# Swin attention half on Trainium2: values twice, V with the projection, centred x with key and variance

## What is computed

```python
def swin_block_fn(x, shift, mask, ...):
    y = layer_norm(x, ln1_g, ln1_b)                       # rolled by -shift, cut into windows
    qkv = wins @ qkv_w + qkv_b
    attn = softmax(q @ k.T * hd ** -0.5 + bias + mask)    # per window and head, 49 x 49
    out = (attn @ v) @ proj_w + proj_b                    # windows back into the image
    x = x + out
    z = layer_norm(x, ln2_g, ln2_b)
    return x + gelu(z @ fc1_w + fc1_b) @ fc2_w + fc2_b
# then, on 4 groups of 16 channels: covariance, 5 Newton steps, out = gamma * wm @ (x - mu) + beta
```

## Time and profile before

| | |
|---|---|
| median of 3 runs | 780.66 us (780.63 to 780.93) |
| profiled execution: time, span | 782.55 us, 780.8 us |
| TensorE busy (matmul) | 693.6 us, 89% |
| TensorE weight loads | 414.3 us, 53% |
| VectorE busy | 534.0 us, 68% |
| ScalarE busy | 357.8 us, 46% |
| POOL busy | 205.0 us, 26% |
| chain that ended last, TensorE's share | 36% |
| attention halves | about 66 to 305 us and 403 to 640 us |

### The profile page before, as it was taken

The page is one execution under the profiler, slowest core; times in us unless marked ns, Lnnn a source line. Parts: engine busy times, 40 slices in busy tenths (PEclk is TensorE's granted clock), DMA queues, the critical chain, the costliest instruction groups (busy, mean ns, idle before and its releaser), DMA issues. The chain is left out here.

```text
span 780.8 us, 27044 instructions
## 1 busy us (share of the span) xinstructions
PE 693.6 (89%) x11574; PEld 414.3 (53%) x11574; DVE 534.0 (68%) x919; ACT 357.8 (46%) x628; POOL 205.0 (26%) x505
## 2 busy tenths in 40 slices
PE   3766999899999998899768999999999987999778
PEld 2633556556666655343334566666566553434557
DVE  1744797788888865787456898887798555782123
ACT  2512455445545544675434455455355444764200
POOL 4000022123222112346500231231122124797000
PEclk9866999999999999999978999999999998999859
DMA  9200121112112111000000121121121110000004
GB/s 228 46 21 21 36 65 55 54 57 68 59 58 69 56 58 38 23 1 1 21 21 25 57 74 54 58 75 52 53 68 61 58 39 23 2 1 1 2 21 144
DMA packets 47627, 37.56 MB, mean 48 GB/s; under 512 B 28564, under 2 KB 47124, under 8 KB 47508
## 3 DMA queue, kind: packets, MB, share of 16 engines
q1 hardware_dynamic: 46496, 33.96, 14.9%
q10 hardware_dynamic: 1012, 1.87, 0.8%
HBM read 18.15 MB, written 4.01 MB: 28 GB/s over the span
## 5 line engine op out<-in xcount | busy, mean ns | idle before, releaser
L423 POOL TENSOR_TENSOR att<-osb,rec 128x392 f32<-128x392 f32 x64 | 71.1, 1111 | 365.5 <-DMA rec<-dens 365.5
L812 DVE TENSOR_REDUCE nmax<-psum 113x16 f32<-113x784 f32 x128 | 117.6, 959 | 42.7 <-PE psum L1024 42.5
L532 ACT ACTIVATE pt<-psum 113x784 f32<-113x784 f32 x128 | 98.6, 824 | 90.5 <-PE psum L1024 90.5
L1024 PE MATMUL psum<-bt,rows_r 117*113 117x392 f32 x256 | 79.0, 409 | 3.9 <-DVE nmax L812 1.2
L838 DVE RECIPROCAL rpk<-dpk 64x49 f32<-64x49 f32 x64 | 28.9, 452 | 53.6 <-DMA dpk<-osb 53.1
L1024 PE MATMUL psum<-pt,vbd 113*32 113x49 f32 x4096 | 59.8, 209 | 3.8 <-ACT osb L539 3.6
L491 ACT ACTIVATE lv<-psum,epsc 128x392 f32<-128x392 f32 x32 | 18.8, 588 | 96.8 <-PE psum L1024 95.6
L416 POOL TENSOR_TENSOR xl<-XW,xh 128x392 fp32r<-128x392 f32 x24 | 31.9, 1329 | 108.3 <-ACT xh L499 108.3
L1024 PE MATMUL psum<-kexp,qsb 32*49 32x196 f32 x2048 | 59.8, 341 | 0.5 <-DMA kexp<-ksb 0.5
L1024 PEld LDWEIGHTS psum<-pt,vbd 113*32 113x32 f32 x4096 | 50.7, 110 | 15.6 <-issue 14.5
L383 POOL TENSOR_TENSOR XW<-XW,wcol 128x49 f32<-128x49 f32 (+5 forms) x200 | 55.3, 314 | 11.8 <-DVE XW L911 11.6
(11 more groups left out here) (174 smaller groups left out, 1221.9 us busy)
## 6 DMA issues: line engine op xcount, KB each, us to landing
rec<-dens SPq DMA_DIRECT2D x64, 196.0 KB
kexp<-ksb SPq DMA_DIRECT2D x128, 49.0 KB
qexp<-qsb SPq DMA_DIRECT2D x128, 49.0 KB
XW<-x_dram SPq DMA_DIRECT2D x14, 196.0 KB, 4.6
out_dram<-XW SPq DMA_DIRECT2D x14, 196.0 KB, 2.4
dpk<-osb SPq DMA_DIRECT2D x64, 12.2 KB
dens<-rpk SPq DMA_DIRECT2D x64, 12.2 KB, 2.6
pt<-w_dram ACTq DMA_DIRECT2D x2, 384.0 KB, 7.6
```

The source lines that it names most:

```text
L423: nc.gpsimd.tensor_tensor(att[:, 4 * part:4 * part + 4, :], osb[part][:, :].rearrange("p (a n) -> p a n", a=4), rec[part][:, :].rearrange( ...
L532: nc.scalar.activation(pt[grp][:, b:b + 2, :], SC[0:KROWS, b:b + 2, 0:BANK], ACT.Exp)\
L812: nc.vector.tensor_reduce(nmax[:, b:b + 2, grp, :], SC[0:KROWS, b:b + 2, 0:BANK].rearrange("p a (k m) -> p a k m", m=NTOK), AX.X, ALU.max, ...
L1024: return nc.tensor.matmul(o, a, b, start=start, stop=stop, **k)
```

## The change

TensorE's `step` gets a new order: `scores_t` part 0, `pv(G-1, 0)` into `bB`, `pv(G-1, 1)` into `bO`, `scores(G+1, 0)`, `f_v(G+1)`, `proj(G-2)` (now in `bO`), `scores(G+1, 1)`, centred x, key, variance, `scores_t` part 1, `maxt`, query (now in `bO`). So the values of part 0 wait for the next step, with a third exponential buffer (`pt_of`). ScalarE makes both output copies behind the exponentials of part 0 and the query's copy behind those of part 1; the variance's copy follows the key's. VectorE takes the row maxima of part 0 before both reciprocals. SP issues both gathers, both stores and both loads in pairs. At the end of the attention half both values of half 15 use `bO`. The projections of the last two halves name `bO`, which is the bank that they had. The numbers of matmuls, their operands and results are the same. Left out of the diff are the bank names in `residual` and the last projections, and the call sites that `f_k` and `f_q` replace in the starts, where the query waits for `rx_done` as before and stays in `bB`.

```diff
@@ -70,7 +70,8 @@
 XW = [sb("XW0", [128, HALVES * TOK]), sb("XW1", [128, HALVES * TOK])]
-ptb = sb("pt", [128, 2, TILES4, BANK])
+ptb = sb("pt", [128, 3, TILES4, BANK])
 ptflat = ptb[:].rearrange("p g b n -> p (g b n)")
@@ -150,7 +151,11 @@
 rx = sb("rx", [128, 2 * GWIN, NTOK], F32R)
-pt = [ptb[0:KROWS, i] for i in range(2)]
+pt = [ptb[0:KROWS, i] for i in range(3)]
+def pt_of(g, grp):
+    return pt[1 if grp else 2 * (g % 2)]
 osb = [sb(f"osb{i}", [128, 4 * NROWS]) for i in range(2)]
@@ -324,16 +329,17 @@
             if G > base:
-                gather(G - 1, 1)
-                to_rows(G - 1, 0)
-                from_rows(G - 1, 0)
-                to_rows(G - 1, 1)
-                from_rows(G - 1, 1)
+                for part in range(2):
+                    gather(G - 1, part)
+                for part in range(2):
+                    to_rows(G - 1, part)
+                for part in range(2):
+                    from_rows(G - 1, part)
             if G + 2 < base + HALVES:
...
                 spread_q(G + 2)
-            gather(G, 0)
         G = base + HALVES - 1
+        gather(G, 0)
         to_rows(G, 0)
@@ -512,7 +518,7 @@
             act.wait_ge(qexp_in[1 - buf], 64 * spread)
-        nc.scalar.activation(qsb[:, :], bB[:, 0:TOK], ACT.Identity, bias=p["vec"][:, QB:QB + 1])\
+        nc.scalar.activation(qsb[:, :], (bB if g1 % HALVES < 2 else bO)[:, 0:TOK], ACT.Identity, bias=p["vec"][:, QB:QB + 1])\
             .then_inc(q_done, 1)
@@ -524,47 +530,47 @@
-    def expo(g, grp, first=False):
+    def expo(g, grp):
         act.wait_ge(st_ready, 2 * g + grp + 1)
-        if not first:
-            act.wait_ge(av_ready, 2 * (g - 1) + grp + 1)
+        if grp and g:
+            act.wait_ge(av_ready, 2 * g)
+        elif g > 1:
+            act.wait_ge(av_ready, 2 * g - 3)
         for b in (0, 2):
-            nc.scalar.activation(pt[grp][:, b:b + 2, :], SC[0:KROWS, b:b + 2, 0:BANK], ACT.Exp)\
+            nc.scalar.activation(pt_of(g, grp)[:, b:b + 2, :], SC[0:KROWS, b:b + 2, 0:BANK], ACT.Exp)\
                 .then_inc(exp_done, 1)
-    def o_copy(g, part, first=False):
+    def o_copy(g, part, bank):
         act.wait_ge(av_ready, 2 * g + part + 1)
-        if not first:
+        if g:
             act.wait_ge(att_done, 2 * (g - 1) + part + 1)
-        nc.scalar.activation(osb[part][:, :], bO[:, 0:4 * NROWS], ACT.Copy).then_inc(osb_done, 1)
+        nc.scalar.activation(osb[part][:, :], bank[:, 0:4 * NROWS], ACT.Copy).then_inc(osb_done, 1)
...
         f = first and base == 0
-        expo(G, 0, f)
+        expo(G, 0)
         if first:
...
         else:
-            o_copy(G - 1, 1, base == 0 and g == 1)
+            o_copy(G - 1, 0, bB)
+            o_copy(G - 1, 1, bO)
         if ahead > 0:
...
             square(G + 3)
-            variance(G + 3, 1 - u)
         if ahead > 1:
             evac_k(p, G + 2, f)
-            evac_q(p, G + 2, u, (G + 1) // 2 + 1)
+        if ahead > 2:
+            variance(G + 3, 1 - u)
         if g + 1 + AHEAD < HALVES:
             x_high(base // HALVES, g + 1)
-        if tail and ahead > 0:
-            tail[1]()
-        expo(G, 1, f)
-        o_copy(G, 0, f)
-        if tail and ahead == 0:
-            tail[1]()
+        expo(G, 1)
+        if ahead > 1:
+            evac_q(p, G + 2, u, (G + 1) // 2 + 1)
@@ -638,10 +644,12 @@
         step(p, base, HALVES - 2, 0, False, 1, pair=PAIRS - 1,
-             tail=[lambda: stats_of(0, m_copy, m_square), lambda: m_variance(0)])
+             tail=[lambda: stats_of(0, m_copy, m_square, m_variance)])
         step(p, base, HALVES - 1, 1, False, 0,
-             tail=[lambda: stats_of(1, m_copy, m_square), lambda: m_variance(1)])
-        o_copy(base + HALVES - 1, 1)
+             tail=[lambda: stats_of(1, m_copy, m_square)])
+        o_copy(base + HALVES - 1, 0, bO)
+        m_variance(1)
+        o_copy(base + HALVES - 1, 1, bO)
         nxt = base + HALVES
@@ -848,10 +856,10 @@
         else:
-            recip(G - 1, 0, blk == 0 and g == 1)
             if ahead > 0:
                 rowmax(G + 1, 0)
-            recip(G - 1, 1, blk == 0 and g == 1)
+            for part in range(2):
+                recip(G - 1, part, G == 1)
         if g > 1:
@@ -1038,12 +1046,14 @@
-    def f_qk(p, g1, buf, free=None):
+    def f_k(p, g1, buf):
...
         mm(bA[:, 0:TOK], p["wk"][:, :], z[buf][:, :]).then_inc(k_ready, 1)
-        pe.wait_ge(*(free or (rx_done, g1)))
-        mm(bB[:, 0:TOK], p["wq"][:, :], z[buf][:, :]).then_inc(q_ready, 1)
+    def f_q(p, buf, bank):
+        mm(bank[:, 0:TOK], p["wq"][:, :], z[buf][:, :]).then_inc(q_ready, 1)
@@ -1098,36 +1108,35 @@
-    def pv(g, grp, buf, first=False):
+    def pv(g, grp, buf, bank):
...
             pe.wait_ge(v_done, 2 * g + 2)
-        if not first:
-            pe.wait_ge(osb_done, 2 * g + grp)
         for win in range(GWIN):
...
                     c0 = (2 * win + hg) * NTOK
-                    last = mm(bO[32 * h4:32 * h4 + 32, c0:c0 + NTOK],
+                    last = mm(bank[32 * h4:32 * h4 + 32, c0:c0 + NTOK],
                               vbd[buf][:, (GWIN * grp + win) * HEADS + 4 * hg + h4, :],
-                              pt[grp][:, h4, c0:c0 + NTOK])
+                              pt_of(g, grp)[:, h4, c0:c0 + NTOK])
         last.then_inc(av_ready, 1)
-    def proj(p, g, bank=bA):
+    def proj(p, g):
...
                 for w in range(2):
-                    last = mm(bank[64 * w:64 * w + 64, 0:TOK].rearrange("p (x i n) -> p x i n", i=2, n=NTOK)[:, :, i],
+                    last = mm(bO[64 * w:64 * w + 64, 0:TOK].rearrange("p (x i n) -> p x i n", i=2, n=NTOK)[:, :, i],
                               p["wph"][:, hh, 64 * i:64 * i + 64], att[:, w::2, hh * NTOK:(hh + 1) * NTOK],
...
-        G = HALVES * blk + g
+        base = HALVES * blk
+        G = base + g
         first = g == 0
@@ -1135,11 +1144,23 @@
         else:
-            pv(G - 1, 1, nb)
+            pv(G - 1, 0, nb, bB)
+            if ahead > 0:
+                pe.wait_ge(q_done, G + 2)
+            else:
+                pe.wait_ge(res_done, G - 2)
+            pv(G - 1, 1, nb, bO)
         if ahead > 0:
+            scores(p, blk, nb, G + 1, 0, lambda i: (exp_done, 4 * G + 1 + i))
             pe.wait_ge(k_done, G + 2)
             f_v(p, nb)
-            scores(p, blk, nb, G + 1, 0, lambda i: (exp_done, 4 * G + 1 + i))
+        if tail:
+            tail[0]()
+        if g > 1:
+            pe.wait_ge(osb_done, 2 * G)
+            proj(p, G - 2)
+        if ahead > 0:
+            scores(p, blk, nb, G + 1, 1, lambda i: (max_done, 4 * G + 5 + i))
         if ahead > 2:
@@ -1148,35 +1169,35 @@
                 f_xc_split(blk, g)
-        if tail:
-            tail[0]()
-        if g > 1:
-            if ahead > 0:
-                pe.wait_ge(v_done, 2 * G + 4)
-            proj(p, G - 2)
-        if ahead > 0:
-            scores(p, blk, nb, G + 1, 1, lambda i: (max_done, 4 * G + 5 + i))
+        if ahead > 1:
+            pe.wait_ge(v_done, 2 * G + 4)
+            f_k(p, G + 2, u)
         if ahead > 2:
...
                 pe.wait_ge(var_used, G + 3)
+            else:
+                pe.wait_ge(osb_done, 2 * G - 1)
             f_var(G + 3)
...
             tail[1]()
-        if ahead > 1:
-            if g > 1:
-                pe.wait_ge(res_done, G - 1)
-            else:
-                pe.wait_ge(v_done, 2 * G + 4)
-            f_qk(p, G + 2, u, (var_used, G + 4) if ahead > 2 else (rx_done, G + 1))
         scores_t(p, blk, u, G, 1, u, pair,
...
         if ahead > 0:
-            if ahead > 1:
-                pe.wait_ge(q_done, G + 3)
+            if ahead > 2:
+                pe.wait_ge(var_used, G + 4)
+            elif ahead > 1:
+                pe.wait_ge(osb_done, 2 * G - 1)
             maxt(G + 1)
-        pv(G, 0, u, first and blk == 0)
+        if ahead > 1:
+            if g > 1:
+                pe.wait_ge(res_done, G - 1)
+            elif g:
+                pe.wait_ge(osb_done, 2 * G)
+            elif blk:
+                pe.wait_ge(mres_done, base)
+            f_q(p, u, bO)
@@ -1336,28 +1360,40 @@
+        def xc_first():
+            pe.wait_ge(osb_done, 2 * G - 3)
+            m_xc(0)
         def var_first():
-            pe.wait_ge(res_done, G - 2)
+            pe.wait_ge(v_done, 2 * G + 2)
             m_var(0)
...
         def xc_second():
+            pe.wait_ge(osb_done, 2 * G - 1)
             m_xc(1)
-            pe.wait_ge(mvar_used, pairs + 1)
...
         def var_second():
-            pe.wait_ge(res_done, G - 1)
+            pe.wait_ge(mvar_used, pairs + 1)
             m_var(1)
-        step(p, blk, HALVES - 2, 0, 1, pair=PAIRS - 1, tail=[lambda: m_xc(0), var_first, copied])
-        step(p, blk, HALVES - 1, 1, 0, pair=PAIRS - 1, tail=[xc_second, spread_first, var_second])
-        pv(G, 1, 1)
+        def nothing():
+            pass
+        step(p, blk, HALVES - 2, 0, 1, pair=PAIRS - 1, tail=[xc_first, var_first, copied])
```

(7 more changed lines are left out.)

23 lines of the change are left out of this document (14 added, 9 removed).

## The result

The changed kernel takes 788.28 us (median of 20 executions, 785.49 to 794.94), the kernel before 782.4 us beside it (20 executions, 777.50 to 790.86): ratio 1.0075, 95% interval 1.0048 to 1.0101. The forecast was 769.3 with a range of 762 to 779, so it is wrong in sign.

The account below looks back on a forecast made before the run. TensorE's instruction order was taken as the bound. 24 steps at 14.3 gave -14.5 us; hiccups +1.5, bias tables +3.6, late steps +0.3, step 0 -6 and half's end +3.8 made -11.3: 769.3 from 780.66, range 762 to 779.

Parts of the forecast that it names:

- switch price: TensorE, between matmul groups of different tile form: each change of form costs up to 0.20 us.
- quiet step: One undisturbed attention step on TensorE: 14.25 us when its groups are added up, 14.3 with an allowance for late row maxima.
- rival (b): TensorE's 0.20 us is an unhidden weight load, not tile form; grouping saves nothing, step 14.65, kernel 777.8 us; chance 0.05.
- wait for the exponentials: TensorE, third bias matmul before the next first scores: the idle wait grows from 0.33 to 0.7 us, the end stays.
- the one for the square: TensorE, variance behind the key: 0.65 us plus 0.2 (0 to 0.35) waiting for its square, made beside the key alone.
- bias tables: VectorE, block 0: two extra tables, some 2 us each in steps without slack there, add 3.6 us (0 to 4).
- Values twice: 0.85, then without a switch 0.74: TensorE, both value parts back to back behind the scores: the second takes 0.74 us (0.70 to 0.85), saving a switch.
- rival (c): VectorE becomes the bound, its late root under POOL's products delaying the maxima; step 14.95, kernel 785 us; chance 0.12.
- Steps 13 and 14: Late attention steps of the blocks: less work to fill the exponential's wait, +0.3 us (0 to 1.6).
- Step 0: First attention step: second scores run inside the gap before centred x, 3 us saved per block (2 to 4), -6 for both.
- End of the attention half: Last value parts share a bank and SP takes the last gather late: 1.9 us per block (0.5 to 2.5), +3.8 together.
- The maxima now come first, so such stalls go: VectorE, row maxima ahead of the reciprocals: stalls from a late gather, 3.30 us idle in one case, disappear.

## Why the prediction was wrong

**Bound and switch price: right.** TensorE's order sets the step, and the quiet step is 14.27 for 14.25 walked. The switches cost what the earlier trace rows said: rival (b) is out, the second values took 1.55 - 0.85 = 0.70 for 0.74. The wait for the exponentials (by the ends of query and bias, 466.75 and 468.09, less the 0.72 that the bias needs, 0.62 for 0.7) and the one for the square (the variance ends 463.86 - 462.94 = 0.92 behind the key, forecast 0.85) were as written. With wide values, where the instructions keep up, the 24 steps take 344.8; the forecast had 343.2 + 1.5 and 3.6 for bias tables. The arithmetic of the step would have held.

**The failed step** is "Values twice: 0.85, then without a switch 0.74". It took from the rows that 128 matmuls can follow each other at the pace of 64. No row of the kernel before shows more than 192 records of 49 and 196 columns together, and the prediction asked for 320 without a bound for it. In its place the runs show that TensorE stands 0.4 to 1.5 us in or just behind this group in 12 of the 24 steps. That is 15.5 to 16.6 of the 18.9 us, by the runs with the earlier spread (3.4 left for it) and with wide values; by the waits themselves the weight loads' "issue" is 15.8 longer than with wide values. The late spread maximum is rival (c) in a weak form. VectorE's timeline of the changed kernel shows what holds it at times; two operations of the root take twice their 0.6 us while POOL multiplies:

```profile
526.11 1.26 DVE L799 TENSOR_TENSOR lt<-lt,lv 128x392 f32<-128x392 f32 x1
527.40 1.27 DVE L800 SCALAR_TENSOR_TENSOR lt<-lt 128x392 f32<-128x392 f32 x1
```

None of the rivals had the instruction stream in it, though the table of waits had an "issue" row for the kernel before, and the page of the profile its own line for instruction packets.

**The other terms.** Steps 13 and 14: +2.8 for +0.3; with wide values +1.5, so about half is the stream again, the rest is left open. Step 0: -3.7 for -6. The order is worth 2.2 to 2.4 us per block where the clock comes back at the same moment, inside the bounds of 2 to 4, for 3 taken; the rest of the difference is that the profiled kernel before had its clock back early in block 1 and the changed kernel late in both. How much of it the second scores bring alone isn't shown. End of the attention half: the two long stretches give +0.8 for +3.8, below the bounds of 1 to 5, but they hold the MLPs and the whitening too. From the start of step 15 to the end of the last output copy it is +1.2 in block 0 and +0.3 in block 1, for 1.9 each: right in direction, too large. Bias tables: in the run with wide values block 0's 12 steps are 172.96 and block 1's 171.84, so at most 1.1 for 3.6.

**Right effect, one of two ways.** "The maxima now come first, so such stalls go": they went. Either edit alone takes them away, the maxima's place (the matmuls' waits for row maxima 7.4 to 2.1 us) as well as the pairing (to 2.5). But the maxima's place without the pairing makes the kernel slower, through SyncE's queue, which the prediction had followed for the change as a whole but not for its parts. The hiccups of the kernel before (8.0 us) were the easier gain: the prediction counted them as a by-product of the new order, and SyncE's four lines alone take them.

What stays open: what makes a packet late. Between the packet's start at 469.5 and the resumption at 472.31 lie 2.8 us; the packet itself takes 1.37 of them, and whether TensorE's sequencer asks too late or the memory answers slowly, and what the time from its end to the resumption (1.2 to 1.6 us everywhere) is made of, can't be read from these traces.

## What to carry to other kernels

Before putting small matmuls side by side, count the instructions, weight loads included, that then fall into two or three microseconds, and compare with the densest group that the trace already shows without an "issue" gap. Where one engine issues several DRAM round trips in order, write them all and then read them all: four lines moved gave 1.8% here (ratio 0.9824, 0.9789 to 0.9859), which beats both kernels. A good order on one engine can pay for a bad one elsewhere; take a change apart before keeping or dropping it.
